# Experts written out step by step, feed-forward tokens normalised on GpSimd, in one two-layer kernel

## The reference

```python
x = x + L0_xattn(layernorm(x), ctx)      # 16 heads of 32, causal
x = x + L0_ffn(layernorm(x))             # 512 -> 2048 -> 512, quantised
x = x + L1_xattn(layernorm(x), ctx)      # 16 heads, latent context
x = x + L1_ffn(layernorm(x))             # experts

def L0_ffn(x):                            # bitlinear: tokens to 8 bits, weights to -1, 0, 1
    h = silu(bitlinear(x, W1))
    return bitlinear(h, W2)
def act_quant(x):
    scale = 127 / clip(max(|x|, per token), 1e-5)
    return clip(round(x * scale), -128, 127) / scale

def L1_ffn(x):                            # 8 experts of 16 units, the best 2 of a token
    weights = softmax(x @ router_w.T)
    gate = weights * top2_mask(weights)
    a = silu(x @ down_w[e].T)
    return sum_e gate[e] * (a @ up_w[e].T)
```

## Time and profile before

| | |
|---|---|
| median of three runs | 1177.27 us |
| profiled execution | 1180.87 us |
| its span, first to last instruction | 1178.9 us |
| PE busy | 1001.1 us (85%) |
| DVE busy | 790.7 us (67%) |
| ACT busy | 654.2 us (55%) |
| POOL busy | 184.3 us (16%) |
| feed-forward stage | 341 to 502 us |
| experts stage | 1077 us to the end |

### The profile page before, as it was taken

One profiled execution on the slowest core, in us unless ns is written; L12 is line 12 of the kernel. 1 busy time (PEld: TensorE's weight loads), 2 busy tenths in 40 slices (PEclk: granted clock), 3 DMA queues, 4 the chain that ended last, 5 costly groups with the idle time before them and its releaser, 6 DMA issues. The chain is left out here.

```text
span 1178.9 us, 20926 instructions
## 1 busy us (share of the span) xinstructions
PE 1001.1 (85%) x7516; PEld 783.9 (66%) x7516; DVE 790.7 (67%) x1729; ACT 654.2 (55%) x1687; POOL 184.3 (16%) x183
## 2 busy tenths in 40 slices
PE   0789999998129989786999999999999999995763
PEld 0778888876114444344888888888878888884652
DVE  5467776664768889625666777677767767674663
ACT  2477777765457776545545555555545545542542
POOL 0555555443000000012001010101001010000000
PEclk9999999998659999998999999999999999997887
DMA  6400000000437000051000000000000000000011
GB/s 236 157 6 7 6 6 7 1 2 1 143 105 234 0 0 0 1 197 37 19 1 19 2 19 1 21 1 4 16 3 18 1 1 1 1 1 1 18 54 71
DMA packets 19679, 41.79 MB, mean 35 GB/s; under 512 B 896, under 2 KB 4224, under 8 KB 19072
## 3 DMA queue, kind: packets, MB, share of 16 engines
q1 hardware_dynamic: 16944, 32.14, 8.4%
q10 hardware_dynamic: 2640, 8.39, 1.9%
HBM read 36.33 MB, written 4.19 MB: 34 GB/s over the span
## 5 line engine op out<-in xcount | busy, mean ns | idle before, releaser
L1322 ACT ACTIVATE probs<-c_score,c_neg_max 128x256 f32<-128x256 f32 x256 | 119.1, 481 | 15.9 <-DVE c_neg_max L1383 14.0
L1308 ACT ACTIVATE c_h<-c_bank_b 128x512 fp32r<-128x512 f32 x64 | 38.2, 597 | 153.7 <-PE c_bank_b L1240 153.7
L526 POOL TENSOR_TENSOR a_probs<-a_probs,a_inv 128x256 f32<-128x256 f32 (+1 forms) x128 | 102.7, 828 | 107.4 <-DVE a_inv L584 107.4
L434 ACT ACTIVATE a_probs<-a_s,a_neg_max 128x128 f32<-128x128 f32 (+1 forms) x256 | 104.0, 433 | 26.6 <-DVE a_neg_max L572 26.0
L1096 POOL TENSOR_TENSOR c_ctx_raw<-c_ctx_raw,c_table 128x1024 f32<-128x1024 f32 x8 | 19.1, 2383 | 597.9 <-PE c_bank_b L1240 357.6
L1373 DVE TENSOR_TENSOR c_l<-c_bank_b,c_h 128x512 fp32r<-128x512 f32 x64 | 44.2, 691 | 99.2 <-ACT c_h L1308 99.2
L44 PE MATMUL c_acc<-VO_h,c_l 128*128 128x512 f32 x256 | 100.8, 394 | 1.9 <-DVE c_l L1373 1.9
L1313 ACT ACTIVATE c_pT_h<-c_turn 128x512 fp32r<-128x512 f32 x128 | 69.7, 596 | 55.6 <-PE c_turn L1230 55.6
L46 PE MATMUL c_acc<-VO_h,c_h 128*128 128x512 f32 x256 | 100.5, 393 | 0.0
L45 PE MATMUL c_acc<-VO_l,c_h 128*128 128x512 f32 x256 | 100.0, 391 | 0.0
L1378 DVE TENSOR_TENSOR c_pT_l<-c_turn,c_pT_h 128x512 fp32r<-128x512 f32 x128 | 81.8, 679 | 2.6 <-ACT c_pT_h L1313 2.6
(11 more groups left out here) (250 smaller groups left out, 2784.9 us busy)
## 6 DMA issues: line engine op xcount, KB each, us to landing
g_x<-in_x ACTq DMA_DIRECT2D x4, 1024.0 KB, 15.8
w_raw<-in_w ACTq DMA_DIRECT2D x1, 4096.0 KB, 14.1
w_raw<-in_w SPq DMA_DIRECT2D x4, 1024.0 KB, 9.1
wq<-in_wq SPq DMA_DIRECT2D x1, 4096.0 KB, 23.0
c_ctx_raw<-in_ctx SPq DMA_DIRECT2D x8, 512.0 KB, 3.4
wo<-in_wo SPq DMA_DIRECT2D x1, 4096.0 KB, 14.2
out<-g_x SPq DMA_DIRECT2D x8, 512.0 KB, 2.8
aw_raw<-in_wq SPq DMA_DIRECT2D x1, 1024.0 KB, 7.7
```

The costliest lines, as they stand in the source:

```text
L434: last = act.activation(probs[i % 2][:, 2 * pair + j, at], s[:, 2 * pair + j, at], ACT.Exp, bias=neg_max[:, pair, q, j:j + 1], accum_out=s ...
L526: last = pool.tensor_tensor(p, p, inv[:, pair, q, :].unsqueeze(2).broadcast_to([P, 2, (q + 1) * P]), ALU.mult)
L1322: last = act.activation(probs[p % 2][:, i, :], score[h][:, t, :], ACT.Exp, bias=neg_max[:, i:i + 1], accum_out=sums[:, i:i + 1])
```

## The change

Feed-forward: the loop is written out (16 tiles as constants), the normalised tile y is doubled and made on GpSimd, and the statistics go to their place without a copy. Experts: everything is written out for each batch, y, yT, weights, gates and gated units are doubled, the expert output has three single-tile banks, the deviations are computed inside the same block, GpSimd does the normalisation, the gating and the low halves of the weights, the two best experts are found on logits before the exponentials, the steps are put in another order, and the output leaves tile by tile. Nothing else is touched: both attentions are the same lines.

```diff
-            for t in range(-3, 1):
-                step(t, t % 2, t)
-            with eng.Fori(0, (TILES - 4) // 2) as r:
-                step(2 * r + 1, 1, None)
-                step(2 * r + 2, 0, None)
-            for t in range(TILES - 3, TILES):
-                step(t, t % 2, t)
+            for t in range(-3, TILES):
+                step(t, t % 2)
...
+            @block.gpsimd
+            def _(pool):
+                for t in range(TILES):
+                    after(pool, x_quant, t - 1)
+                    pool.tensor_scalar(y[t % 2][:, :], X[:, t, :], mv[:, t, 0:1], rstd[:, t:t + 1], ALU.subtract, ALU.mult
+                                       ).then_inc(y_ready, 1)
...
                 def quantise_tokens(t, par):
                     after(dve, x_turned, t - 1)
-                    dve.tensor_scalar(y[:, :], X[:, bass.ds(t, 1), :].rearrange("p a d -> p (a d)"),
-                                      mv[:, bass.ds(t, 1), 0:1].rearrange("p a d -> p (a d)"),
-                                      rstd[:, bass.ds(t, 1)], ALU.subtract, ALU.mult)
-                    dve.drain()
-                    dve.tensor_reduce(amax[:, 0:1], y[:, :], AX.X, ALU.max, apply_absolute_value=True)
+                    dve.wait_ge(y_ready, t + 1)
+                    dve.tensor_reduce(amax[:, 0:1], y[par][:, :], AX.X, ALU.max, apply_absolute_value=True)
...
                 def new_stats(t):
-                    xt = X[:, bass.ds(t, 1), :].rearrange("p a d -> p (a d)")
-                    tile_stats(dve, xt, stats[:, :], new_mv[:, :])
-                    dve.drain()
-                    dve.tensor_copy(mv[:, bass.ds(t, 1), :].rearrange("p a d -> p (a d)"), new_mv[:, :])
+                    tile_stats(dve, X[:, t, :], stats[:, :], mv[:, t, :])
...
+                for s in steps:
+                    if 0 <= s + 1 < B:
+                        hidden_units(s + 1)
+                    if 0 <= s - 1 < B:
+                        expert_out(s - 1)
+                    if 0 <= s < B:
+                        turn_gated(s)
+                    if 0 <= s + 3 < B:
+                        turn_y(s + 3)
...
+                for s in steps:
+                    if 0 <= s + 1 < B:
+                        weights(s + 1)
+                        activate(s + 1)
+                    if 0 <= s < B:
+                        split_gated(s)
+                    if 0 <= s + 3 < B:
+                        split_y(s + 3)
...
+                def normalise(b):
+                    if b >= 2:
+                        pool.wait_ge(turned, b - 1)
+                    normalise_y(pool, b).then_inc(y_ready, 1)
+
+                def apply_gates(b):
+                    pool.wait_ge(gated, b + 1)
+                    pool.wait_ge(acted, b + 1)
...
+                    pool.tensor_tensor(units, units, gates, ALU.mult).then_inc(g_ready, 1)
+
+                pool.wait_ge(rstd_ready, 1)
+                normalise(1)
+                pool.wait_ge(wd_hi, 1)
+                pool.tensor_tensor(wd_l[:, :, 0:GE], wd[:], f32(wd_h[:, :, 0:GE]), ALU.subtract).then_inc(wd_lo, 1)
...
+                for s in steps:
+                    if 0 <= s < B:
+                        apply_gates(s)
+                    if 2 <= s + 4 < B:
+                        normalise(s + 4)
...
+                def choose(b):
+                    dve.wait_ge(hid, b + 1)
+                    if b > 0:
+                        dve.wait_ge(exped, b)
+                    dve.tensor_copy(logits[:], hidden[b % 2][:, :, G:GE])
+                    dve.drain()
+                    for t in range(TPB):
+                        dve.max(top[:, t, :], logits[:, t, :])
+                    dve.drain()
+                    dve.tensor_scalar(neg_max[b % 2][:, :], top[:, :, 0], -1.0, None, ALU.mult).then_inc(maxed, 1)
...
+                for s in steps:
+                    if 0 <= s + 2 < B:
+                        b = s + 2
+                        dve.wait_ge(y_hi, b + 1)
+                        dve.tensor_tensor(yT_l[b % 2][:], turn[:], f32(yT_h[b % 2][:]), ALU.subtract).then_inc(y_lo, 1)
+                    if 0 <= s < B:
+                        gates(s)
+                    if 0 <= s + 1 < B:
+                        choose(s + 1)
+                    if 0 <= s - 1 < B:
+                        for tile in range((s - 1) * TPB, s * TPB):
+                            dve.wait_ge(upped, tile + 1)
+                            dve.tensor_tensor(X[:, tile, :], X[:, tile, :], up[tile % UP][:, :], ALU.add).then_inc(added, 1)
+                    if 0 <= s < B:
+                        dve.wait_ge(g_hi, s + 1)
+                        dve.tensor_tensor(g_l[s % 2][:, :], turn_g[:, 0:TPB * P], f32(g_h[s % 2][:, :]), ALU.subtract
+                                          ).then_inc(g_lo, 1)
```

More of the change, by code:

```diff
@@ L857, in _, with step @@
             def _(act):
[L858 to L859 removed]
+                def step(t, par):
+                    if has(t, 0):
                         for i in range(2):
@@ L1531, in _, with hidden_units @@
-                all_steps(pe, step)
+                def hidden_units(b):
+                    pe.wait_ge(y_lo, b + 1)
+                    if b == 0:
+                        pe.wait_ge(wd_lo, 2)
+                    h, l = yT_h[b % 2], yT_l[b % 2]
+                    for t in range(TPB):
+                        last = products(pe, hidden[b % 2][:, t, :], [(h[:, t, c, :], l[:, t, c, :], wd_h[:, c, :], wd_l[:, c, :])
+                                                                     for c in range(DC)])
+                    last.then_inc(hid, 1)
@@ new lines, in expert_out @@
+                def expert_out(b):
+                    pe.wait_ge(g_lo, b + 1)
+                    if b == 0:
+                        pe.wait_ge(wu_lo, 1)
+                    for t in range(TPB):
+                        tile, tok = b * TPB + t, slice(t * P, (t + 1) * P)
+                        if tile >= UP:
+                            pe.wait_ge(added, tile - UP + 1)
+                        products(pe, up[tile % UP][:, :], [(g_h[b % 2][:, tok], g_l[b % 2][:, tok], wu_h[:, :], wu_l[:, :])]
+                                 ).then_inc(upped, 1)
@@ L1533, in _ @@
+                for s in steps:
[7 more added lines that the diff above has]
+                        turn_y(s + 3)
             @block.scalar
             def _(act):
-                def step(b, par, at):
-                    if has(at, 2):
-                        act.wait_ge(turned, b + 3)
-                        act.activation(yT_h[:], turn[:], ACT.Copy).then_inc(y_hi, 1)
-                    if has(at, 0):
-                        act.wait_ge(g_turned, b + 1)
-                        act.activation(g_h[:, :], turn_g[:, 0:TPB * P], ACT.Copy).then_inc(g_hi, 1)
-                    if has(at, 1):
-                        act.wait_ge(maxed, b + 2)
-                        for t in range(TPB):
-                            act.activation(weight[:, t, :], hidden[1 - par][:, t, G:GE], ACT.Exp, bias=neg_max[:, t:t + 1],
-                                           accum_out=sums[:, t:t + 1])
-                        act.drain().then_inc(exped, 1)
-                        act.activation(act_h[:], hidden[1 - par][:, :, 0:G], ACT.Silu).then_inc(acted, 1)
@@ L1549, in _, with weights @@
-                act.wait_ge(expert_in, 3 * DMA)
-                act.activation(wd_h[:, :, GE:WIDTH], wd[:, :, 0:WIDTH - GE], ACT.Copy)
-                act.activation(wd_h[:, :, 0:GE], wd[:], ACT.Copy).then_inc(w_hi, 1)
-                act.activation(wu_h[:], wu[:], ACT.Copy).then_inc(w_hi, 1)
-                all_steps(act, step)
+                def weights(b):
+                    act.wait_ge(maxed, b + 1)
+                    if b >= 2:
+                        act.wait_ge(gated, b - 1)
+                    for t in range(TPB):
+                        act.activation(weight[b % 2][:, t, :], hidden[b % 2][:, t, G:GE], ACT.Exp,
+                                       bias=neg_max[b % 2][:, t:t + 1], accum_out=sums[b % 2][:, t:t + 1])
+                    act.drain().then_inc(exped, 1)
@@ L1603, in step @@
-                def step(b, par, at):
-                    if isinstance(b, int) and b == -2:
-                        split_weights()
-                    if has(at, 1):
-                        dve.wait_ge(hid, b + 2)
-                        dve.tensor_reduce(neg_max[:, :], hidden[1 - par][:, :, G:GE], AX.X, ALU.max, negate=True).then_inc(maxed, 1)
-                    if has(at, 2):
-                        dve.wait_ge(y_hi, b + 3)
-                        dve.tensor_tensor(yT_l[:], turn[:], f32(yT_h[:]), ALU.subtract).then_inc(y_lo, 1)
-                    if has(at, 0):
-                        dve.wait_ge(g_hi, b + 1)
-                        dve.tensor_tensor(g_l[:, :], turn_g[:, 0:TPB * P], f32(g_h[:, :]), ALU.subtract).then_inc(g_lo, 1)
-                    if has(at, 3):
-                        normalise_y(b + 3)
-                    if has(at, 1):
```

(6 more changed lines are left out.)

234 lines of the change are left out of this document (120 added, 114 removed).

## The result

The changed kernel takes 1141.58 us (median of 4 runs, 1137.67 to 1142.64), the kernel before 1176.90 beside it: ratio 0.9686, interval 0.9666 to 0.9705. Forecast were 1138.0 us and 1130 to 1152. The profiled execution is 1142.28 us with a span of 1140.4, where the forecast's sum had 1141.6.

The account below looks back on a forecast made before the run. Feed-forward was taken as paced by VectorE, experts by a chain of waits. Profiled 1180.87 - 10.7 (feed-forward) - 28.6 (experts) = 1141.6; the median lies 3.6 lower: 1138.0 us, range 1130 to 1152.

Parts of the forecast that it names:

- The change touches two stages: Opening premise: only feed-forward and experts change; the sum has no term for any other stage.
- Step 8.07: Feed-forward: each tile step falls from 8.94 to 8.07 us, TensorE setting the pace; twelve steps gain 10.4 us.
- the tail: Feed-forward's last tiles: VectorE starts its addition about 1.1 us earlier and has no copy; 1.2 us gained.
- The head: Feed-forward start: tile 0 waits for GpSimd's normalisation, 1.5 us lost, 0.6 won back in two steps; 0.9 net loss.
- First maxima: Experts start: the router's first row maxima (d_neg_max) stand at 1093.6 us, against 1091.47 in the kernel before.
- the ring: Experts: ScalarE (3.65) and VectorE (2.7) alternate between sets of maxima, 6.4 us a step; second maxima after 6.0.
- its bound of 31: Experts: most that could be gained, 31 us, with 6.1 us between maxima and full clock throughout.
- From the last maxima to the end: Experts: last chain of gates, turning, products, addition and output takes 12.3 us, ending at 1150.3.
- own range: Main case: feed-forward gains 8 to 12 us, experts 25 to 31, giving 1131 to 1145 us; 76%.
- B: Experts: TensorE stays at 1.2 GHz and becomes the bound, 20 us more, 1158; 9%, halfway case 1148, 7%.
- C: GpSimd and VectorE shut each other out during GpSimd's normalisations in both stages; slower, 1192 us; 4%.
- D: Feed-forward: the saving is swallowed by waiting for ScalarE's b_hr at 8.6 us; 4 of 10.7 remain, 1145; 4%.

Follow-up runs that it names:

- loop_hinted: The changed kernel with the jump back of TensorE's second-attention loop announced; ratio 0.9631 (0.9582-0.9680) to the kernel before.

## Why the prediction was right, and where it was not

**The sum.** 1141.6 in the profiled frame against 1142.3 measured. The parts: feed-forward 1.2 and experts 3.2 us better than said, 3.15 of scatter in the first attention, and +8.4 that the sum did not have. Right to 0.7 us by luck: three errors of the forecast and the scatter of one execution cancel. The offset of 3.6 us between the profiled execution and the median shrank to 0.7, which makes the rest of the distance to 1138.0.

**The step that failed** is the sentence "The change touches two stages", at the start of the prediction. It changes lines of two, but TensorE's instructions behind the written-out one moved. The sum has no term for the second attention, which puts it at nothing without a reason. It should have had one with bounds. By what the runs showed, a jump cost 1.3 us before and up to 5.6 after, so two jumps lose up to 8.6 us more. The trace of before had the hint, 65.2 against 63.9 wherever the loop jumps; I did not read the untouched stages.

**Feed-forward, point by point.** Step 8.07 said, 8.02 measured, TensorE at the pace as said. VectorE's own work is 8.02 - 0.26 = 7.76 a step, said 7.7. Twelve steps gave 10.95 (10.4 said) and the tail 1.0 (1.2). The head: tile 0's first transposes of hidden units came 1.54 us later after the start, as said (1.5), and the next step was 1.54 shorter, so it cost nothing net where 0.9 was said. Attribution was partly wrong: the step was reasoned with the normalisation (0.62) as the largest saving, but behind the writing out it was worth 0.24 a step, since TensorE then has the pace.

**Experts, point by point.** First maxima 15.0 us into the stage (16.0 said). From first to last 41.1 (44.4 said): the ring is 6.16, not 6.4, and the last interval is 4.4, since the last pair has no yT_h and yT_l of a later pair to make. The prediction counted seven alike bar the first. For that reason the 31.8 us also lie above its bound of 31, which had the ring at 6.1. From the last maxima to the end 13.4 (12.3 said); in front of the last gates stands an addition of 1.28 us that I had not put there. The members of the ring were right as far as tried: with the table loads out the step shrank by 0.9, down to TensorE's own need.

**Rivals and range.** The lower end of the own range does not follow from its parts: 12 and 31 us gained make 1134, not the 1131 written. B is seen only as single steps of 7.7 to 7.8 us in some executions; after has 1.00 granted through the ring. Over the whole stage it is 0.84, against the sign of "over 0.9": the stretch up to the second maxima (1070.9 to 1091.7) is granted 0.70 and the last chain (from 1127) 0.66. C holds in its mechanism and not in its place. GpSimd's first two normalisations meet b_yr of VectorE, which then takes 0.96 us in place of 0.49 and ends only behind them:

```profile
337.98 4.13 POOL L879 TENSOR_SCALAR b_y<-g_x,g_mean_var,g_rstd 128x512 f32<-128x512 f32 x2 [35.27 <-POOLq L706]
```

```profile
341.42 0.96 DVE L910 TENSOR_SCALAR b_yr<-b_y,b_q_scale 128x512 f32<-128x512 f32 x1
```

In the steady steps b_hq is first, and it is GpSimd that takes 2.98 in place of 2.07, which nobody waits for: the argument of the prediction for its 4% was the order, and the order held. The Trainium skill (GPSIMD Engine Reference, 8. Key points) makes no exception for a one-input normalisation, and for these two VectorE instructions the trace agrees with it (b_yr 0.96 in place of 0.49, GpSimd 2.98 in place of 2.07 beside b_hq); whether they run in the 2-port mode that it names, no trace shows. The 0.42 us of the earlier trace rows, on which I leaned, is another VectorE instruction, and it stands as the case that disagrees. D did not occur.

## What to carry to other kernels

Writing a loop out moves everything behind it, on every engine whose code grew: list the loops that follow, and in the trace compare the intervals that hold a jump back with those that don't; a wait on "issue" behind the jump is its sign, and placing the loop's head early in a block, announcing the jump or writing the loop out took most or all of TensorE's loss away here. Read every stage of before and after, not only the changed ones. And when an engine is no longer the pace, taking more off it gains nothing: moving the normalisation to GpSimd was worth 1.6 us in the one stage and nothing in the other. Writing out gave the rest in the feed-forward; in the experts the parts of the rewrite were not tried one by one.

## What the runs showed of the hardware that I had not expected

- A jump back on TensorE cost, by the places counted in the built program, 1.0 to 1.5 us with the head at place 201 of a block of 256, 4.6 to 5.9 at place 240 (5.7 and 2.6 at 236), and 0 to 0.8 in most jumps at place 16, with single ones of 1.7 and 3.4. Of the 5.6 at the first jump after, 3.5 are the two waits, the rest the low clock behind them and what the other engines wait.
- In seven jumps of the kernels with the head at place 16 or the jump announced, the instruction queue fetched no block for a whole iteration, and TensorE waited for none; in the others of place 16 it fetched, and the interval was 0.5 to 3.4 us longer.
- GpSimd's normalisation of 128x512 takes 2.07 us, 2.98 when it starts beside VectorE's b_hq (1.22), and holds b_yr up when it is first (0.96 in place of 0.49). In loop_hinted VectorE's scaling of the probabilities took 3.27 us in place of 1.14 beside GpSimd's L1092.
